# The moments of a last normalisation taken on ScalarE and GpSimd, and exponentials stored with the head innermost, in an attention and product-key kernel

## The reference

```python
def _layernorm(x, axis=-1, eps=1e-05):
    m = jnp.mean(x, axis=axis, keepdims=True)
    v = jnp.var(x, axis=axis, keepdims=True)
    return (x - m) / jnp.sqrt(v + eps)

# product-key layer, n tokens, 8 heads, 32 keys for each of two halves
sim = jnp.einsum('pbnhd,hkpd->pbnhk', q, keys)
sx, ix = jax.lax.top_k(sim[0], 8)
sy, iy = jax.lax.top_k(sim[1], 8)
all_scores = sx[..., :, None] + sy[..., None, :]     # 64 pairs for each head
scores, pk = jax.lax.top_k(all_scores, 8)
h = gelu_new(jnp.einsum('bnd,bnhkd->bnhk', x, down_embed[indices]))
h = jax.nn.softmax(scores, axis=-1) * h
out = jnp.einsum('bnhk,bnhkd->bnd', h, up_embed[indices])

x = _layernorm(x + attention_part(x))
x = _layernorm(x + product_key_part(x))
```

## Time and profile before

| what | value |
|---|---|
| median of 3 runs | 785.1 us (784.61, 785.1, 792.95) |
| profiled execution | 780.71 us, span 778.8 us |
| busy, PE / DVE / ACT / POOL | 618.8 / 609.4 / 346.9 / 436.8 us |
| mean granted clock of TensorE | 0.937 |
| busy between 597 and 607 us, PE / DVE / ACT / POOL | 7.75 / 9.68 / 5.21 / 8.79 of 10 us |

### The profile page before, as it was taken

One profiled execution on the slowest core, in us unless ns is written; L12 is line 12 of the kernel. 1 busy time (PEld: TensorE's weight loads), 2 busy tenths in 40 slices (PEclk: granted clock), 3 DMA queues, 4 the chain that ended last, 5 costly groups with the idle time before them and its releaser, 6 DMA issues.

```text
span 778.8 us, 46654 instructions
## 1 busy us (share of the span) xinstructions
PE 618.8 (79%) x19783; PEld 513.8 (66%) x19783; DVE 609.4 (78%) x1879; ACT 346.9 (45%) x546; POOL 436.8 (56%) x680
## 2 busy tenths in 40 slices
PE   5888979999998977888547587677888777777784
PEld 4677868778877855556346476566777666676674
DVE  3566657776766757999855888899999999999982
ACT  3344534545444452655430444445554445455540
POOL 4222422333232323556521878878988888988881
PEclk9999999999999998999865689999999999999998
DMA  7511111111111110000000222322222222222221
GB/s 175 193 33 38 31 29 33 35 35 33 33 37 28 32 56 14 15 28 13 0 8 7 45 55 66 68 49 61 66 67 67 67 61 67 67 64 60 61 57 37
DMA packets 45362, 38.82 MB, mean 50 GB/s; under 512 B 6512, under 2 KB 40432, under 8 KB 45040
## 3 DMA queue, kind: packets, MB, share of 16 engines
q1 hardware_dynamic: 45296, 37.86, 19.4%
HBM read 16.86 MB, written 2.10 MB: 24 GB/s over the span
## 4 chain that ended last, share of the span: by engine, by line
PE 45%; DVE 36%; issue 15%; POOL 2%; ACT 1%; DVEq 1%; POOLq 0%; ACTq 0%
PE ps L651 12%; PE ps L664 8%; DVE top L1239 5%; PE ps L677 5%; PE ps L838 5%; DVE prod L1294 4%; PE ps L817 3%; DVE wq_sb L1270 3%; PE ps L646 3%; DVE r L1078 3%; DVE stats L1058 2%; DVE best L1250 2%; DVE r_x L1279 2%; DVE hidT L1285 2%; PE ps L826 2%
## 5 line engine op out<-in xcount | busy, mean ns | idle before, releaser
L1017 DVE TENSOR_REDUCE row_max<-ps 128x8 f32<-128x768 f32 x64 | 61.3, 958 | 77.4 <-PE ps L651 77.4
L838 PE MATMUL ps<-up_sb,prod 128*128 128x128 f32 x512 | 79.6, 317 | 48.0 <-DVE prod L1294 47.3
L465 POOL COPY v_ones<-v_raw 96x512 f32<-96x512 f32 x32 | 19.5, 609 | 169.4 <-DMA v_raw<-in_x_wrapped 160.1
L875 ACT ACTIVATE arena<-arena 128x768 f32<-128x768 f32 x64 | 54.0, 844 | 125.3 <-DVE arena L1020 125.3
L838 PEld LDWEIGHTS ps<-up_sb,prod 128*128 128x128 f32 x512 | 73.1, 224 | 54.6 <-DVE prod L1294 53.7
L651 PE MATMUL ps<-early 128*32 128x96 f32 x4096 | 103.3, 252 | 5.8 <-issue 5.7
L651 PEld LDWEIGHTS ps<-early 128*32 128x32 f32 x4096 | 87.8, 112 | 28.7 <-issue 28.7
L817 PE MATMUL ps<-arena,hidT 128*32 128x32 f32 x8192 | 81.7, 200 | 26.2 <-issue 21.2
L817 PEld LDWEIGHTS ps<-arena,hidT 128*32 128x32 f32 x8192 | 76.7, 112 | 31.6 <-issue 22.8
L568 POOL TENSOR_TENSOR wq_sb<-wq_sb,rel_exp 128x1024 f32<-128x1024 f32 x32 | 76.3, 2384 | 8.4 <-POOL rel_exp L564 7.0
L859 ACT ACTIVATE arena<-ps 96x512 f32<-96x512 f32 x128 | 68.6, 585 | 26.6 <-PE ps L664 26.5
(11 more groups left out here) (140 smaller groups left out, 1285.3 us busy)
## 6 DMA issues: line engine op xcount, KB each, us to landing
arena<-r_x SPq DMA_DIRECT2D x128, 128.0 KB, 2.4
v_raw<-in_x_wrapped SPq DMA_DIRECT2D x128, 48.0 KB, 1.8
arena<-in_x SPq DMA_DIRECT2D x8, 256.0 KB, 4.9
x_tile<-in_x SPq DMA_DIRECT2D x32, 64.0 KB, 1.7
x<-in_x SPq DMA_DIRECT2D x8, 256.0 KB, 2.8
xT_tile<-xT SPq DMA_DIRECT2D x32, 64.0 KB, 1.9
out<-out_tile SPq DMA_DIRECT2D x32, 64.0 KB, 1.6
wq_sb<-in_w_q SPq DMA_DIRECT2D x1, 1024.0 KB, 9.6
```

What stands on the lines that cost most here:

```text
L838: mm = nc.tensor.matmul(ps[:, 6 + p, 0:P], pairs[:, c // 2, c % 2], up_sb[:, c, :], start=False, stop=(c == EC - 1))
L1017: V.tensor_reduce(mx.rearrange("p (a b) -> p a b", a=2), sc, AX_X, ALU.max).then_inc(max_done, 1)
```

## The change

Three things are done.

1. The mean and variance of the last normalisation leave VectorE (`last_moments` is gone). ScalarE adds the 128 columns with a copy that has a sum output (`last_sum`), GpSimd makes minus the mean of it (`last_mean`), ScalarE adds the squares of the deviations with a second activation (`last_square`), and GpSimd scales that and adds epsilon ahead of its power (`last_scale`).
2. On GpSimd `last_mean` stands between `classes` of the tile and `thresholds` of the next one. On ScalarE `last_sum` stands between the two kinds of exponentials, `last_square` ahead of `last_norm`.
3. `rel_exp` is stored as half, key, head. ScalarE writes it turned, and GpSimd's operations read it in order.

```diff
--- before.py
+++ after.py
@@ -175,7 +175,7 @@
         rz = two("rz", [P, PK_HEADS])
 
         limits = two("limits", [P, PK_HEADS, 10])
-        rel_exp = two("rel_exp", [P, PH, KEYS])
+        rel_exp = two("rel_exp", [P, 2, KEYS, PK_HEADS])
 
         def halves(flat):
             return [flat[:, p * EXPERTS:(p + 1) * EXPERTS] for p in range(2)]
@@ -191,8 +191,10 @@
         act = [early[:, p * EXPERTS:(p + 1) * EXPERTS] for p in range(2)]
         gated = halves(prod[:].rearrange("p a d -> p (a d)"))
         out_tile = two("out_tile", [P, P])
-        stats4 = sb("stats4", [P, 6])
-        mom4 = sb("mom4", [P, 2])
+        scratch = sb("scratch", [P, P])
+        sum4 = sb("sum4", [P, 1])
+        minus_mean4 = sb("minus_mean4", [P, 1])
+        square4 = sb("square4", [P, 1])
         var4 = sb("var4", [P, 1])
         rstd4 = sb("rstd4", [P, 1])
         shift4 = sb("shift4", [P, 1])
@@ -560,12 +563,12 @@
                 pool.wait_ge(rz_done, t + 1)
                 pool.wait_ge(relexp_done, t + 1)
                 hold(pool)
-                ey = rel_exp[p][:, PK_HEADS:PH, :]
-                nc.gpsimd.tensor_tensor(ey, ey, bcast(rz[p][:], 2, KEYS), ALU.mult).then_inc(scaled, 1)
+                ey = rel_exp[p][:, 1]
+                nc.gpsimd.tensor_tensor(ey, ey, bcast(rz[p][:], 1, KEYS), ALU.mult).then_inc(scaled, 1)
                 pool.wait_ge(scaled, t + 1)
                 pool.wait_ge(masked, 2 * t + 1)
                 hold(pool)
-                nc.gpsimd.tensor_tensor(right[p], right[p], bcast(ey.rearrange("p h j -> p j h"), 3, TERMS), ALU.mult
+                nc.gpsimd.tensor_tensor(right[p], right[p], bcast(ey, 3, TERMS), ALU.mult
                                         ).then_inc(right_ready, 1)
 
             def classes(t, p):
@@ -578,18 +581,27 @@
             def scale_left(t, p):
                 pool.wait_ge(classes_done, t + 1)
                 hold(pool)
-                ex = rel_exp[p][:, 0:PK_HEADS, :].rearrange("p h i -> p i h")
+                ex = rel_exp[p][:, 0]
                 nc.gpsimd.tensor_tensor(left[p][:, :, :, 0:TERMS - 1], left[p][:, :, :, 0:TERMS - 1],
                                         bcast(ex, 3, TERMS - 1), ALU.mult).then_inc(left_ready, 1)
 
+            def last_mean(t):
+
+                pool.wait_ge(d_sum, t + 1)
+                hold(pool)
+                nc.gpsimd.tensor_scalar(minus_mean4[:], sum4[:], -1.0 / P, 1.0, ALU.mult, ALU.mult).then_inc(d_mean, 1)
+
             def last_scale(t):
 
-                pool.wait_ge(d_var, t + 1)
+                pool.wait_ge(d_square, t + 1)
+                hold(pool)
+                nc.gpsimd.tensor_scalar(var4[:], square4[:], 1.0 / P, EPS, ALU.mult, ALU.add).then_inc(rstd_step, 1)
+                pool.wait_ge(rstd_step, 2 * t + 1)
                 hold(pool)
                 nc.gpsimd.tensor_tensor(rstd4[:], var4[:], minus_half[:, 0:1], ALU.pow).then_inc(rstd_step, 1)
-                pool.wait_ge(rstd_step, t + 1)
-                hold(pool)
-                nc.gpsimd.tensor_scalar(shift4[:], mom4[:, 0:1], rstd4[:], -1.0, ALU.mult, ALU.mult).then_inc(d_rstd, 1)
+                pool.wait_ge(rstd_step, 2 * t + 2)
+                hold(pool)
+                nc.gpsimd.tensor_tensor(shift4[:], minus_mean4[:], rstd4[:], ALU.mult).then_inc(d_rstd, 1)
 
             def d_pool(i):
                 for p in range(2):
@@ -600,6 +612,8 @@
                         tops(t + 1, o)
                     if have(t):
                         classes(t, p)
+                    if have(t - 2):
+                        last_mean(t - 2)
                     if have(t + 1):
                         thresholds(t + 1, o)
                     if have(t):
@@ -959,8 +973,18 @@
             def rel_exps(t, p):
                 a.wait_ge(rel_done, t + 1)
                 need(a, left_ready, t - 1)
-                nc.scalar.activation(rel_exp[p][:].rearrange("p a k -> p (a k)"), ps[:, p, :], ACT.Exp
+                nc.scalar.activation(rel_exp[p][:].rearrange("p a k h -> p a h k"),
+                                     ps[:, p, :].rearrange("p (a h k) -> p a h k", a=2, h=PK_HEADS), ACT.Exp
                                      ).then_inc(relexp_done, 1)
+
+            def last_sum(t, p):
+                a.wait_ge(up_done, t + 1)
+                nc.scalar.activation(scratch[:], ps[:, 6 + p, 0:P], ACT.Copy, accum_out=sum4[:]).then_inc(d_sum, 1)
+
+            def last_square(t, p):
+                a.wait_ge(d_mean, t + 1)
+                nc.scalar.activation(scratch[:], ps[:, 6 + p, 0:P], ACT.Square, bias=minus_mean4[:], accum_out=square4[:]
+                                     ).then_inc(d_square, 1)
 
             def last_norm(t, p, i):
                 a.wait_ge(d_rstd, t + 1)
@@ -975,8 +999,12 @@
                     t, o = 2 * i + p, 1 - p
                     if have(t + 1):
                         rel_exps(t + 1, o)
+                    if have(t - 2):
+                        last_sum(t - 2, p)
+                    if have(t + 1):
                         best_exps(t + 1, o)
                     if have(t - 2):
+                        last_square(t - 2, p)
                         last_norm(t - 2, p, i - 1)
                     if have(t + 1):
                         gelus(t + 1, o)
@@ -1294,16 +1322,6 @@
                     V.tensor_tensor(out4[:, :, half], ps[:, 2 + half, :].rearrange("p (j x) -> p j x", j=EC // 2),
                                     act4[:, :, half], ALU.mult).then_inc(gated_done, 1)
 
-            def last_moments(t, p):
-                v.wait_ge(up_done, t + 1)
-                V.bn_stats(stats4[:], ps[:, 6 + p, 0:P]).then_inc(d_step, 1)
-                v.wait_ge(d_step, 2 * t + 1)
-                need(v, out_ready, t)
-                hold(v)
-                V.bn_aggr(mom4[:], stats4[:]).then_inc(d_step, 1)
-                v.wait_ge(d_step, 2 * t + 2)
-                V.tensor_scalar(var4[:], mom4[:, 1:2], EPS, None, ALU.add).then_inc(d_var, 1)
-
             v.wait_ge(x3_kept, NQ)
 
             def d_dve(i):
@@ -1311,8 +1329,6 @@
                     t, o = 2 * i + p, 1 - p
                     if have(t + 1):
                         top_keys(t + 1, o)
-                    if have(t - 2):
-                        last_moments(t - 2, p)
                     if have(t):
                         turn_right(t, p, i)
                     if have(t + 1):
```

7 lines of the change are left out of this document (4 added, 3 removed).

## The result

After takes 792.27 us (median of four runs, 788.93 to 797.26), before 784.86 beside it: the ratio is 1.0099, 95% interval 1.0053 to 1.0145. Run again, with a profile of its own, the ratio was 1.0123 (1.0074 to 1.0171). The forecast was 780.0, a little faster; the kernel became 1% slower.

What follows compares the result with a forecast made beforehand. VectorE and GpSimd were both taken as full, with a loop through both setting 9.85 us a tile: 19 tiles -3.8, three low-clock tiles -1.8, early tiles -0.4, end +0.9, together -5.1 us, giving 780 us (777.5 to 783.5).

Steps and rivals of the forecast that it cites:

- What bounds the tile: Last stage: VectorE (10.05 us a tile) and GpSimd (10.07) are both full, so taking 0.8 us from VectorE alone gains nothing.
- GpSimd 9.74 us a tile: GpSimd's work per last-stage tile: 10.07, plus 0.60 for new steps, minus 0.93 from the new layout.
- the line from L531 to L575: GpSimd products: 0.19 us fixed plus 1.66 ns per element; L568's and L582's excess of 0.50 and 0.53 taken as gone.
- rival B: GpSimd's two products run at L489's rate, layout gains only 0.25 us, GpSimd 10.42 a tile, 793 us; chance 0.12.
- The loop 9.84: Chain from tile to tile through GpSimd and VectorE, new step included: 9.84 us, longest of three, taken as the period.
- The rule of the Trainium skill: GpSimd reads stepping over 8 bytes cost about 2.9 cycles an element, not 1.9; read to the letter, layout gains nothing.
- ScalarE: Two added activations at 0.45 us each and a spread store at +0 to +0.1; the sum arrives with 0.2 to spare.
- rival C: ScalarE's sum comes late through a slow spread store or sum read-out, GpSimd waits ahead of L551, 788 us; chance 0.08.
- The end: The last tile's path from L1299 to L589, without cover, grows from 1.04 to 1.93 us: +0.9.
- Three took about 11.0 to 11.1: Three of 22 last-stage tiles run longer because TensorE's granted clock fell; the other nineteen took 10.05 us.
- the sum's 3 x -0.6: The three tiles with a low TensorE clock each save 0.6 us on the path from maxima to gate: -1.8.
- The last sentence of the prediction: Prediction is wrong if GpSimd has another loop wait, or TensorE, idle less, has its clock lowered in over three tiles.

Runs made afterwards that it cites:

- e5: After with the mean and variance steps moved from GpSimd to ScalarE and the exponentials in the old layout; 787.9 us, ratio 1.0053 to before.
- e1: Before with only the new layout of the exponentials, moments still on VectorE; 786.5 us, ratio 1.0009 to before.
- e9: Before plus one unused one-column instruction on GpSimd ahead of the thresholds; 785.7 us, ratio 1.0022 to before.
- e12: Before plus three unused one-column instructions on GpSimd ahead of the thresholds; 793.4 us, ratio 1.0137 to before.
- e2: After with the exponentials back in the old layout, so only the moments are moved; 805.0 us, ratio 1.0223 to before.
- e3: After with minus the mean made by ScalarE's summing activation and GpSimd's `last_mean` removed; 786.3 us, ratio 1.0001 to before.
- e14: After plus two unused TensorE matmuls ahead of the wait for the gate; 788.4 us, ratio 0.9988 to before.
- e13: Before plus two unused TensorE matmuls ahead of the wait for the gate; 787.8 us, ratio 1.0006 to before.
- e17: After plus three unused TensorE matmuls ahead of the wait for the gate; 787.1 us, ratio 0.9986 to before.
- e15: After with the whole last normalisation on ScalarE, the old layout and two unused TensorE matmuls ahead of the gate wait; 773.2 us, ratio 0.9773 to before.
- e18: After with the whole last normalisation on ScalarE, the new layout and two unused TensorE matmuls ahead of the gate wait; 769.9 us, ratio 0.9795 to before.
- e19: After with the exponentials in the old layout, plus two unused TensorE matmuls ahead of the gate wait; 800.0 us, ratio 1.0161 to before.

## Why the prediction was wrong, step by step

**What bounds the tile**: right. Two full engines; VectorE relieved alone gives nothing (e5), GpSimd relieved alone gives nothing (e1), GpSimd loaded alone is paid for in the tile (e9, e12).

**GpSimd 9.74 us a tile**: this is the term of the sum that was mis-sized. The layout gave 0.35 on L568 and 0.28 from start to start on L582, 0.63 in all, not 0.93. The reading that the whole excess over the line from L531 to L575 goes with the operand that jumps was too kind: L568 now takes 2.03 us where the line has 1.89, L582 1.60 where it has 1.47. What is left, 0.14 and 0.13, is again the same for 1024 and 768 elements, so it isn't a rate like that of L489 (rival B), which would leave 0.45 and 0.33. Reading 256 neighbouring values costs 0.27 in both together, where 0.1 was allowed. The other 0.13 is lost behind L582: before, the next instruction starts 0.04 ahead of its end, now 0.08 behind it (L598, the new step). The scaling L564 was not in the sum and costs 0.11 more: its 1/z, before the same for 32 elements in a row, now changes with every element. `last_mean` 0.28 instead of 0.20, the variance step 0.38 (predicted 0.40). That makes 10.07 - 0.63 + 0.11 + 0.28 + 0.38 - 0.06 (the shift) = 10.15, and 10.15 was measured. With it the undisturbed tile is 0.1 longer instead of 0.2 shorter. By the prediction's sum the 22 tiles take 224.1 - 3.8 - 1.8 = 218.5 us; they took 231.8, 13.3 more, and 22 x 0.3 = 6.6 of that is this term. Its size lay between the forecast and rival B, the mechanism was the forecast's.

**The loop 9.84**: right in size (e2 shows 9.84, e3 9.57 without the new step), but not the longest of the three, so not the period.

**The rule of the Trainium skill** (GPSIMD Engine Reference, section 7) was weighed in two readings, of the inner step or of the head's. The runs side with the head's in part: in e1 nothing else changed, and the operations fell by 0.38 and 0.40 us.

**ScalarE**: the store's step costs 0.51 us where at most 0.1 was allowed for, rival C's condition. In undisturbed tiles it costs nothing, because GpSimd comes later too. Behind a fall, where the loop rules, it does: L592 waited eight times, 0.2 to 0.3 us each, 1.9 in all, and those tiles take 9.97 to 10.12 us where e2, with the quick store, has 9.84. So C's wait is there, but not in the tiles that the forecast was about.

**The end**: +0.7 measured, +0.9 predicted.

**"Three took about 11.0 to 11.1"**, and the sum's 3 x -0.6: this step failed by the rest of the 13.3. It took the count of before as given, at 10.45 us, 0.6 above an undisturbed tile, 1.8 in all. After has eight, at 0.5 to 2.1 us each above an undisturbed tile, 8.5 in all, 6.7 more than in the sum and 5.5 more than in before. The last sentence of the prediction named it as a danger, but for the wrong reason (TensorE idle for less time). With the same filler and two low tiles each, after and before are equal (0.9988 and 1.0006, e14 and e13), and without a low tile after takes 0.9986 of before (e17). Of the seven kernels with a filled hole four have no low tile (e15 to e18), e14 has two where after has eight, e13 keeps two of three and e19 eight of eleven. So filling the hole takes falls away, and all of the loss of after with them; it doesn't take all of them away everywhere, and e9 lost its falls without it. The undisturbed tile alone (10.13 against 10.05) would be 2 us, within the interval.

**What stays open** is why after has eight falls and before three. The length of the wait at the gate doesn't decide it. The waits of after, of e9 and of e3 (total us, times, longest; over 216, 220 and 228 us of the row):

```profile
PE ps L852 <- DVE prod L1322: 38.2, 20, 2.4
```

```profile
PE ps L841 <- DVE prod L1297: 48.5, 22, 2.5
```

```profile
PE ps L850 <- DVE prod L1320: 35.0, 22, 1.9
```

e9 waits longest and has no low tile among its 22; e3 waits least and has eleven, each with a wait of 1.8 to 1.9 us. Nor has after the larger hole to begin with: 2.13 to 2.16 us in undisturbed tiles, where before has 1.9 and 2.2 in turn. What differs is what follows a fall. In after the next tile waits 1.2 or 1.3 us and the one behind it 2.3 or 2.4, and six of the eight falls come in such a tile; in before the wait behind a fall is 1.6 to 1.9, then 1.9 to 2.2, and no tile is hit again so soon. I take it that a row in which a fall lengthens the wait two tiles on can go on by itself, and that how the row of tiles lies in time decides the rest. Neither was tried by itself.

## What to carry to other kernels

When two engines are both full, sum up each of them for the new order from start to start, and put every instruction whose access pattern changes into the sum, those that get slower too. Where TensorE has a hole of a microsecond or two in every round of a loop, look at the granted clock of each tile ahead of the change and after it, and at that of all runs, since the number of falls differs between executions: a change elsewhere can shift the number of falls and with it more time than the change itself is worth. A little work without a use in the hole, placed ahead of the wait, is a cheap test, and here, once GpSimd had been relieved as well, also the largest gain.
